# Class-token values of layers 1 to 3 in two parts, and four weight chunks in front of the second stacks of each layer's first pass

## The reference, cut to what matters

```
for i in range(L):                       # L = 4 layers
    q, k, val = split(h @ W_qkv[i])      # h: 8 images x 257 rows x 256
    AC = (q + u) @ k^T ; BD = (q + v) @ (r @ W_r[i])^T
    prob = softmax((AC + BD) / 8)
    vec  = prob @ val
    h = layer_norm(h + vec @ W_o[i], ln1_g[i], ln1_b[i])
    ff = relu(h @ W_ff1[i] + b_ff1[i]) @ W_ff2[i] + b_ff2[i]
    h = layer_norm(ff, ln2_g[i], ln2_b[i])
```

## Time and profile before

| what | us |
|---|---|
| median of three runs | 2495.08 |
| the profiled execution | 2493.25 |
| its span, first to last instruction | 2491.4 |
| TensorE busy | 2223.1 (89%) |
| VectorE busy | 1833.0 (74%) |
| ScalarE busy | 1607.2 (65%) |
| GpSimd busy | 1175.8 (47%) |

### The profile page before, as it was taken

One profiled execution on the slowest core, in us unless ns is written; L12 is line 12 of the kernel. 1 busy time (PEld: TensorE's weight loads), 2 busy tenths in 40 slices (PEclk: granted clock), 3 DMA queues, 4 the chain that ended last, 5 costly groups with the idle time before them and its releaser, 6 DMA issues.

```text
span 2491.4 us, 61244 instructions
## 1 busy us (share of the span) xinstructions
PE 2223.1 (89%) x19318; PEld 1660.7 (67%) x19318; DVE 1833.0 (74%) x5685; ACT 1607.2 (65%) x4899; POOL 1175.8 (47%) x2201
## 2 busy tenths in 40 slices
PE   0289999999989999999989999999899999988998
PEld 0257777777767777777667777777677777765655
DVE  8667777777767787777767777777678888886533
ACT  3257777776667777776667777777677777774322
POOL 1046555554556555555555555554566555541101
PEclk9889999999999999999999999999999999999999
DMA  3564444445554444444644444445543334345110
GB/s 118 140 172 116 106 107 112 113 129 155 132 158 123 111 109 111 106 123 144 180 118 114 113 110 113 121 135 146 158 106 97 94 100 109 99 136 187 54 46 23
DMA packets 378059, 295.35 MB, mean 119 GB/s; under 512 B 45087, under 2 KB 350721, under 8 KB 376739
## 3 DMA queue, kind: packets, MB, share of 16 engines
q1 hardware_dynamic: 370603, 272.41, 41.8%
q10 hardware_dynamic: 4864, 12.68, 1.5%
q0 software_dynamic: 2272, 6.35, 0.7%
HBM read 137.45 MB, written 72.07 MB: 84 GB/s over the span
## 4 chain that ended last, share of the span: by engine, by line
PE 33%; ACT 24%; DVE 12%; POOL 8%; SPq 7%; issue 6%; DMA 4%; DVEq 0%; POOLq 0%; ACTq 0%
ACT e_rows L2168 11%; PE bk L2066 5%; PE bk L2078 5%; SPq L1532 4%; PE bk L1272 4%; ACT p_flat L2150 4%; PE bk L2035 4%; PE bk L1906 3%; DVE x L2425 3%; DVE o_rows L2333 3%; ACT rel L2099 2%; POOL arena L1727 2%; PE bk L1894 2%; POOL arena L1725 2%; PE bk L1845 2%
## 5 line engine op out<-in xcount | busy, mean ns | idle before, releaser
L2168 ACT ACTIVATE e_rows<-e_rows,nb 128x257 f32<-128x257 f32 x1024 | 516.1, 515 | 34.9 <-DVE nb L2362 34.2
L2362 DVE CUSTOM_DVE_ANT_0 e_rows<-bk,arena 128x257 f32<-128x257 f32 x1024 | 390.1, 418 | 72.0 <-PE bk L1940 70.7
L1845 PE MATMUL bk<-hin,arena 128*128 128x257 f16 x3072 | 422.0, 274 | 16.7 <-DMA hin<-hd_dram 11.1
L2324 DVE TENSOR_TENSOR p_flat<-bk,p_flat 128x512 f16<-128x512 f32 x512 | 353.8, 691 | 66.7 <-ACT p_flat L2150 54.2
L1894 PE MATMUL bk<-ident,e_rows 128*128 128x128 f32 x2048 | 324.9, 281 | 51.8 <-ACT e_rows L2168 29.3
L1727 POOL TENSOR_TENSOR arena<-rel,arena 128x257 f16<-128x257 f32 x496 | 328.3, 662 | 41.4
L1845 PEld LDWEIGHTS bk<-hin,arena 128*128 128x128 f16 x3072 | 296.4, 97 | 67.4 <-issue 18.6
L1725 POOL TENSOR_SCALAR arena<-rel 128x257 f16<-128x257 f32 x496 | 203.7, 411 | 265.1 <-ACT rel L2099 258.4
L2150 ACT ACTIVATE p_flat<-bk 128x512 f16<-128x512 f32 x512 | 310.0, 605 | 7.9 <-PE bk L1894 7.9
L1894 PEld LDWEIGHTS bk<-ident,e_rows 128*128 128x128 f32 x2048 | 222.4, 141 | 136.9 <-ACT e_rows L2168 115.3
L1775 POOL TENSOR_SCALAR wf<-wf 128x256 f32<-128x256 f32 x216 | 94.1, 436 | 363.9 <-DMA wf<-in_w_dram 187.7
(11 more groups left out here) (327 smaller groups left out, 4232.8 us busy)
## 6 DMA issues: line engine op xcount, KB each, us to landing
arena<-arena SPq DMA_DIRECT2D x768, 128.5 KB, 3.5
wf<-in_w_dram SPq DMA_DIRECT2D x168, 128.0 KB, 2.8
w_split_dram<-wh SPq DMA_DIRECT2D x168, 128.0 KB, 2.4
xs_dram<-in_c_blank_dram SPq DMA_DIRECT2D x24, 772.5 KB
wf<-in_we_dram SPq DMA_DIRECT2D x96, 128.0 KB, 2.6
we_split_dram<-wh SPq DMA_DIRECT2D x96, 128.0 KB, 1.9
w_rest<-w_split_dram SPq DMA_DIRECT2D x12, 1024.0 KB, 17.2
arena<-we_split_dram SPq DMA_DIRECT2D x8, 1536.0 KB, 12.0
```

The costliest lines, as they stand in the source:

```text
L1845: r_ = mm(bank[4 + s % 2][:, 0:S], wcol(a, C_QKV, k, 3 * HD, chunk_at(s)), hin[:, m, k, :], start=i == 0, stop=i == 5)
L2168: act.activation(E[:, h % EB, qt, :], E[:, h % EB, qt, :], ACT.Exp, bias=nb[:, 2 * h + qt:2 * h + qt + 1], scale=-1.0, accum_out=sums[:, q ...
L2324: v.tensor_tensor(pt[:, h, 1, :, 0:IMG], bank[2 + h % 2][:, :].rearrange("p (k s) -> p k s", k=QT), pt[:, h, 0, :, 0:IMG], ALU.subtract).t ...
L2362: v.tensor_tensor_reduce(E[:, h % EB, qt, :], bank[qt][:, 0:S], cb[:, h, :], -SCORE, 3e38, ALU.add, ALU.min, nb[:, 2 * h + qt:2 * h + qt + ...
```

## The change

In layers 1 to 3 the class values are computed in two parts. Part one, in pass b = 0, does images 0 to 6 (seven columns of `hcls`); part two, in pass b = 1, does image 7 (one column). Both stand in head 5 on TensorE, head 6 on ScalarE and head 7 on VectorE. SP stores each part as soon as it is made, with three DMAs, ahead of the pass's first stacks; in the entry pass `load_vbd` stands right behind the first stacks, and the store of the layer output behind that. The compressed order of the second layer norm in the entry pass is gone; it goes as in the other passes. In the entry pass SP handles chunks 0 to 3 ahead of the second stacks, chunks 4 and 5 behind them, and then the loads of `vbd` and `hin`, with six chunks left for after these (three before the change). The diff, cut to its core:

```diff
+        FIRST_IMAGES = slice(0, B - 1)
+        LAST_IMAGE = slice(B - 1, B)
+        class_images = lambda l, b: slice(0, B) if l == 0 else (FIRST_IMAGES, LAST_IMAGE)[b]
+        class_count = lambda l, b: 2 if l == 0 else 4 * l + 2 * b
+        class_due = lambda l, b: l > 0 and b < 2
...
-            def store_vcls(atl):
-                hold(vcls_lo, atl(2, 2))
+            def store_vcls(l, b):
+                hold(vcls_lo, class_count(l, b))
+                images = class_images(l, b)
                 for copy, t in enumerate((0, 0, 1)):
-                    sp.dma_start(vbd_diagonal(io["vbd"], copy), vcl[:, t, :]...
+                    sp.dma_start(vbd_diagonal(io["vbd"], copy)[images],
+                                 vcl[0:images.stop - images.start, t, :]...
...
             def load_vbd(g):
-                hold(vbd_out, 48 * (g // B + 1))
+                hold(vbd_out, 24 * class_count(g // B, int(g % B == B - 1)))
...
+                if class_due(l, b):
+                    store_vcls(l, b)
                 if kind.next and not kind.closing:
                     stack(at1, 0)
+                if kind.entry:
+                    load_vbd(at.g)
                 if kind.ln2 and not kind.routes:
                     store(at, (B if kind.entry else b) - 1)
                 if kind.closing:
                     stack(at1, 0)
-                if kind.entry:
-                    store_vcls(At(sp, l))
-                    load_vbd(at.g)
+                first_chunks = 4 if kind.entry else 0
+                for c in range(first_chunks):
+                    store_chunk(c)
                 if kind.next:
                     stack(at1, 1)
...
-                late = max(len(plan) - 3, 0)
-                for c in range(late):
+                late = max(len(plan) - (6 if kind.entry else 3), 0)
+                for c in range(first_chunks, late):
                     store_chunk(c)
...
# GpSimd, second layer norm
-                        early = kind.entry
-                        if not early and h in (4, 5):
+                        if h in (4, 5):
                             ln2_normalise(at, h - 4)
-                        if not early and h in (6, 7):
+                        if h in (6, 7):
                             ln2_gain(at, h - 6)
-                        if early and h == 4:
...
-                        if h in ((6, 7) if early else (9, 10)):
-                            ln2_lo(at, h - (6 if early else 9))
-                        if h == (7 if early else 10):
+                        if h in (9, 10):
+                            ln2_lo(at, h - 9)
+                        if h == 10:
                             ln2_class(at, (B if kind.entry else b) - 1)
...
# TensorE
-                        r_ = mm(bank[6 + half][0:B, :], hcls[:, m, k, :], ...
+                        r_ = mm(bank[6 + half][0:images.stop - images.start, :], hcls[:, m, k, images], ...
...
-                    if h == NP + 1 and kind.entry:
-                        pe.wait_ge(hcls_ok, atl(8, 0))
+                    if h == 5 and class_due(l, b):
+                        pe.wait_ge(hcls_ok, 8 * l - 1 + b)
+                        pe.wait_ge(vy_ok, at(1, 0))
                         pe.wait_ge(pc_lo, at(1, 1))
-                        class_v()
+                        class_v(l, b)
...
-                if kind.entry:
-                    pe.wait_ge(vcls_lo, atl(2, 2))
+                if class_due(l, b):
+                    pe.wait_ge(vcls_lo, class_count(l, b))
                 pv(at, 0)
...
# ScalarE
-                    if kind.ln2 and h in ((6, 7) if kind.entry else (8, 9)):
-                        ln2_hi(at, h - (6 if kind.entry else 8))
+                    if h in (8, 9) and kind.ln2:
+                        ln2_hi(at, h - 8)
...
-                    if h == NP + 2 and kind.entry:
-                        class_v(atl)
+                    if h == 6 and class_due(l, b):
+                        class_v(l, b)
...
+                if l and b == 1:
+                    act.wait_ge(vbd_out, 24 * class_count(l, b))
                 for c in range(NP):
                     act.wait_ge(rb_done, at(8, c + 1))
...
# VectorE
-                    if h == NP + 3 and kind.entry:
-                        class_v(atl)
+                    if h == 7 and class_due(l, b):
+                        class_v(l, b)
```

More of the change, by code:

```diff
@@ L1514, in hold @@
                 sp.wait_ge(signal, n)
-            def store_vcls(atl):
-                hold(vcls_lo, atl(2, 2))
+            def store_vcls(l, b):
+                hold(vcls_lo, class_count(l, b))
+                images = class_images(l, b)
                 for copy, t in enumerate((0, 0, 1)):
-                    sp.dma_start(vbd_diagonal(io["vbd"], copy), vcl[:, t, :].rearrange("b (h d) -> b h d", h=H)).then_inc(vbd_out, 16)
+                    sp.dma_start(vbd_diagonal(io["vbd"], copy)[images],
+                                 vcl[0:images.stop - images.start, t, :].rearrange("b (h d) -> b h d", h=H)).then_inc(vbd_out, 16)
             def stack(at, part):
@@ L1682, in _ @@
             sp.wait_ge(zero_out, 16)
-            store_vcls(At(sp, 0))
+            store_vcls(0, 0)
             sp.wait_ge(first_lo, NP)
@@ L1864, in project_v, with class_v @@
                     r_.then_inc(v_done, 1)
-            def class_v():
+            def class_v(l, b):
+                images = class_images(l, b)
                 for half in range(2):
@@ L1870, in class_v @@
                     for i, (k, (a, m)) in enumerate((k, t) for k in range(KC) for t in TERMS):
-                        r_ = mm(bank[6 + half][0:B, :], hcls[:, m, k, :], w_part(W, a, c0 + k * 3 * HD, c0 + k * 3 * HD + 512),
+                        r_ = mm(bank[6 + half][0:images.stop - images.start, :], hcls[:, m, k, images], w_part(W, a, c0 + k * 3 * HD, c0 + k * 3 * HD + 512),
                                start=i == 0, stop=i == 5)
@@ L1909, in _ @@
             first = At(pe, 0)
-            class_v()
+            class_v(0, 0)
             pe.wait_ge(const_ok, CONST)
@@ L2104, in v_part, with class_v @@
                 act.activation(vs[:, 0, tt, half * 512:half * 512 + 512], bank[VB[u]][:, :], ACT.Copy).then_inc(v_hi, 1)
-            def class_v(atl):
+            def class_v(l, b):
+                n = class_images(l, b).stop - class_images(l, b).start
                 for half in range(2):
-                    act.wait_ge(vcls_done, atl(2, half + 1))
-                    act.activation(vcl[:, 0, half * 512:half * 512 + 512], bank[6 + half][0:B, :], ACT.Copy).then_inc(vcls_hi, 1)
+                    act.wait_ge(vcls_done, class_count(l, b) - 1 + half)
+                    act.activation(vcl[0:n, 0, half * 512:half * 512 + 512], bank[6 + half][0:n, :], ACT.Copy).then_inc(vcls_hi, 1)
             def first_rstd(var_done, n, bk, log_ok, y_ok):
@@ L2139, in _ @@
                 act.dma_start(io["cc"].rearrange("(h s) -> h s", h=H)[4 * j:4 * j + 4, :], cc[32 * j:32 * j + 4, :]).then_inc(cc_out, 16)
-            class_v(first)
+            class_v(0, 0)
             for s in range(0, 2 * NP, 2):
```

12 lines of the change are left out of this document (4 added, 8 removed).

## The result

The median went from 2495.08 us to **2486.41 us** (seven runs each: 2492.88 to 2497.59, and 2482.62 to 2489.57). The ratio is 0.9964 [0.9952, 0.9975]: 8.7 us less, where 9.8 were forecast.

A forecast was written before the change was run, and what follows sets the result against it. ScalarE and TensorE, nearly in step, bound the head loops, with TensorE's `vbd` and `hin` waits on top. Terms -5.1 - 8.5 - 5.0 + 8.8 = -9.8 us gave 2483.45 profiled, 2485.3 median; range 2477 to 2493.

The forecast's parts named there:

- the clock at full: Condition on the entry passes' value stages: TensorE's clock stays up despite a remaining `vbd` wait of 2 to 3 us.
- Entry head loops: Head loops of passes 8, 16, 24: less ScalarE idle and no hurried layer norm, 1.70 us a layer, 5.1 us gained.
- Part two: Image 7's class values in b = 1 head loops cost 2.93 us three times, a loss of 8.8 us.
- The `hin` wait: Start of passes 9, 17, 25: `hin` goes out about 743 instead of 755.81, the wait goes, 5.0 us gained.
- The `vbd` wait: Value stages of entry passes: `vbd` ready at 719.4 instead of 723.2, 8.0 of 16.5 us left, 8.5 us gained.
- a stage clock still at 0.8: Sign that the prediction is wrong: the granted clock of a stage has not risen from 0.8.
- `vbd` hidden altogether: Rival, entry value stages: stacks end before 712.4, `vbd` arrives ahead of TensorE, another 8.0 us go, 2477.3 us; chance 0.15.
- `vbd` no earlier: Rival, entry value stages: loads land behind all stacks, `vbd` at today's time, +3.8 us, 2498.9 us; chance 0.13.
- No slack: Rival, head loops: class work has no slack at its new place, both parts cost 3.9 us, 2491.1 us; chance 0.12.
- `hin` late: Rival, start of passes 9, 17, 25: `hin` still late because SP's queue is, +5.0 us, 2490.3 us; chance 0.05.

The follow-up runs named there:

- second pair: Traces of the kernel before and the kernel after, both unchanged and run again in one set; medians 2495.51 and 2483.3 us.
- d1: Kernel after without part two: image 7's class values of layers 1 to 3 left out, so output is not the reference's; 2478.04 us, ratio 0.9927.
- b1: Kernel before with only SP's chunks moved, four ahead of the second stacks in entry passes; 2490.98 us, ratio 0.9982.
- b2: Kernel after with SP's chunks back at their old place, all nine behind the second stacks; 2492.01 us, ratio 0.9991.
- c1: Kernel after with the third 1 MB weight load moved behind the first stacks and `load_vbd`; 2472.16 us, ratio 0.9906.
- c2: Kernel after with the 772.5 KB of zero rows of passes 7, 15, 23 issued at the end of the pass after; 2474.7 us, ratio 0.9919.
- g3: c4 run again, unchanged, in the third set; 2470.23 us, ratio 0.9901.
- e1: c1 with the class values' two halves in heads 5 and 6 instead of both in head 5, copies and subtractions likewise; 2473.73 us, ratio 0.9913.
- c4: c1 with the entry passes' chunk order in pass 0 too; 2471.61 us, ratio 0.9901.
- second set: Follow-up runs of c2, d1, c4 and e1, with their own runs of the kernel before, median 2495.9 us.
- a1: Kernel after, unchanged, run again in the first set beside the kernel before; 2481.59 us, ratio 0.994.
- g2: Kernel after, unchanged, run again in the third set; 2483.3 us, ratio 0.9962.

## Why the prediction came out as it did

The time, its sign and the mechanism of each term in the sum were right; one condition, the clock at full, was not. That the total fits to about 1 us is partly luck. In the first pair of traces the forecast terms add up to -8.4 us (-6.1 - 6.6 + 4.3) and not to -9.8, and changes that were not in the sum stand beside them (-2.8, +3.8, +3.7); in the second pair it is -8.5, with -2.8, +1.5 and +0.4 beside it. The three sets' medians gave 8.7, 13.4 and 11.2 us. Step by step:

- **Entry head loops: right.** 1.95 us of ScalarE idle at head 6 against a forecast of 1.97, the copies at 1.05, the 0.73 us gone, loops of 32.6 against 32.8. The gain is 6.1 and not 5.1, since passes 16 and 24 gave 1.9 and 2.4 us where pass 8, the one worked out, gave 1.8. More than half of the 1.0 us over the forecast is a term that the prediction left alone, the wait for `hin` at the start of the entry pass: 0.82, 0.80 and 1.28 us before, 0.82, 0.74 and 0.74 after. ScalarE's idle time at head 6 is 1.95 us in all three entry passes. The second pair shows the same, 3.2 us of such waits before and 2.4 after; whether the change or chance shortens them is not shown.
- **Part two: right.** b = 1 head loops of 32.0 against 31.9, and d1 puts the cost at 2.8 us a layer.
- **The `hin` wait: right**, place and mechanism. SP issues `hin` at 743.06 on before's scale, forecast about 743, and b1 removes the wait by this edit alone. Its size depends on the execution: 5.0 us in the first trace of before, 3.0 in the second (89.79 less three times 28.93).
- **The `vbd` wait: the mechanism right, the term too large by 2 us.** Stores at 700.0 (forecast 699.9), stacks ending at 714.8 (714.3), TensorE at the waiting matmul of pass 8 at 717.2 on before's scale (717.4; the row of before gives 719.03, not 719.14, to start from), `vbd` there at 720.2 (719.4), waits of 7.45 us in all (8.0). Singly they fit less well, 3.02, 2.12 and 2.31 against 1.9, 2.7 and 3.4, so the close sum is partly luck. But the excess of the three stages over 14.24 us is 9.96 us, not 8.0: the step that failed is "if the clock stays up". The granted clock of the stages was 0.90, 0.90 and 0.81, and the last of these is one of the recorded signs of being wrong, a stage clock still at 0.8. I had argued from one gap of 2.32 us that did no harm; gaps of 2.1 to 3.0 us did, and cost 9.96 - 7.45 = 2.5 us. The second pair gives a gain of 8.7 for this term: before's stages were 0.9 us longer there and after's 1.2 us shorter (waits of 6.75 us).
- **Not in the sum: -2.8 us** in the stage from the value projections to the first feed-forward product. It is the same in both pairs. In pass 8 the rows show the cause, VectorE beside an idle GpSimd. b2, with the chunks back at their place, has again 6.72 us in this stage of pass 8, and one such VectorE instruction at 0.93 us. Over the three entry passes the stage takes 20.4 us before, 19.6 in b1 (chunks alone), 20.2 in b2 (split alone) and 19.0 with both. So the chunk order, which I priced for SP and `hin` alone, also decides what GpSimd does meanwhile. In the passes b = 1, whose own chunk order nobody changed, it is 20.4 us before, 20.1 in b1, 19.1 in b2 and 19.0 with both (20.0 and 19.4 in the second pair): there the gain comes with the split. GpSimd isn't idle in these (3 us busy of 6.2 in pass 9), its instructions only fall beside others; that this is the cause there is argued and not shown.
- The Trainium skill ("SBUF — State Buffer", Who interferes with whom) says that VectorE and GpSimd share one pair of ports, and that a VectorE instruction with two inputs in this memory contends with a GpSimd instruction that reads it. The 0.43 against 0.64 to 0.93 us of an instruction with two such inputs agrees.

**The rivals.** `vbd` hidden altogether did not happen, and its condition was well put: c1, c2 and g3 lie on the two sides of it. `vbd` no earlier is refuted by the last load, issued by 722.4 and read by the matmul at 724.30, 1.9 us later and not 6.7. No slack is refuted by the 1.95 us. `hin` late is what b2 shows, where the chunks aren't moved.

**The two unforeseen losses in the first profile.** Pass 1 lies in layer 0, where the change alters neither SP's order nor the class values. What its head loop has over 28.9 us is mostly a wait for `hin` (3.1 us in the first profile, 1.5 before), and in the first profile the granted clock of 0.90 beside it. It took 30.2 us in both traces of before, 34.0, 32.1 and 31.7 in the three of after, and 33.9 in b1 and 32.0 in d1; but 30.0 to 30.5 in b2, c1, c2 and e1, which differ from after only in later passes. So no edit to layer 0 explains it, and yet I can't call it chance: c4's chunk order in pass 0 takes the wait away, but what sets its length without that order stays open. The value stages of 7.65 us and more in passes 26 to 30 came in the first profile and in all four kernels of the second set, and in none of the first and third sets, which held the same kernel after. In them ScalarE's first copy behind the first scale matmul starts 0.95 to 1.23 us after it, and 0.31 us after it in all the others; no row names what holds it. They go with the set rather than with the code. Whether the kernel before has them in such a set too can't be said: both its traces have 7.01 us, but none is from the second set, and its first one is from before the change was run. So it is not ruled out that only kernels with the split can show them.

## What to carry to other kernels

Where a small transfer stands behind a row of large ones, look at what the queue is still holding before reordering what stands behind it: here moving one weight load back was worth 9.4 us in the same set, and moving back the 772.5 KB of zero rows that the pass before had issued was worth 5 to 11 us by its ratio, each about as much as the whole change. When work is split to get it off the critical path, price each part by its own streaming time: twelve matmuls cost 2.75 us for eight columns, seven or one, so the second part cost 8.5 us where the entry passes' head loops gained 6.1, and only the earlier `vbd` paid. A gap that is left after a change should be charged with the clock too, not only with its length.

## What was not expected of the hardware

- The clock fell behind `vbd` gaps of 2.12, 2.31 and 3.02 us (granted 0.90, 0.81, 0.90 over the stage) and `hin` gaps of 3.14 us (pass 1, 0.90) and 3.36 us (b2, 0.91), and stayed at full behind a `hin` gap of 2.32 us and a `vbd` gap of 1.35. `hin` gaps of 3.34 us (a1, pass 1) and 3.25 us (d1, pass 1) left it at full as well, while head loops with gaps of 1.81 us (g2, pass 1) and 1.93 us (d1, pass 24) had 0.95. The length of the gap alone did not decide it.
- The issue of the twelve equal DMAs of pass 8 took 8.7 us where the weights ahead of them had landed (c2), 10.3 and 12.0 us behind two weight loads (c1, g3), and 13.0 us behind three. With the pass's start put on before's scale, the weights' last piece ended at 698.9, 706.4, 707.6 and 710.3.
- VectorE's 128x257 two-input instruction took 0.43 us with GpSimd idle and up to 0.93 us beside GpSimd's splitting of a chunk.
